# Tables and projection in one stage, four stored blocks a side, masks and picking rows kept on chip

## The reference

```python
xn = layernorm(x)
q, k, v = xn @ Wq + bq, xn @ Wk + bk, xn @ Wv + bv          # 16 heads of 16
pos = rel_emb @ Wk + bk                                     # 128 rows: one for a bucket of distance
scores = q @ k.T + take(q @ pos.T, c2p_pos) + take(k @ pos.T, p2c_pos).T
out = (softmax(scores / sqrt(48)) @ v) @ Wo + bo + xn
x = x + layernorm(layernorm(out) * ln_scale + ln_bias)
# feed-forward: expert = argmax(layernorm(x) @ Wr + br); relu(. @ W1 + b1) @ W2 + b2; again norm and residual
```

## Time and profile before

| | us |
|---|---|
| median of 3 runs (1906.63 to 1910.41) | 1906.98 |
| the profiled execution | 1909.95 |
| its span, first to last instruction | 1908.0 |
| TensorE busy | 1656.5 (87%) |
| DVE busy | 1390.5 (73%) |
| ScalarE busy | 1151.0 (60%) |
| GpSimd busy | 1071.8 (56%) |
| data moved by DMA | 452.57 MB, 237 GB/s |

### The profile page before, as it was taken

How to read it: one execution, slowest core, us unless ns; L and a number is a source line. 1 busy time by engine, 2 the same in 40 slices (tenths; PEclk the granted TensorE clock), 3 DMA queues, 4 the chain that set the end, 5 groups by cost and what they waited for, 6 DMA issues and landing times. The chain is left out here.

```text
span 1908.0 us, 41019 instructions
## 1 busy us (share of the span) xinstructions
PE 1656.5 (87%) x13688; PEld 1140.5 (60%) x13688; DVE 1390.5 (73%) x3938; ACT 1151.0 (60%) x2745; POOL 1071.8 (56%) x1268
## 2 busy tenths in 40 slices
PE   1883289999999999999999999999944755999997
PEld 1442056666666666666666666666523645999996
DVE  1573099999999999999999999999823652434343
ACT  1673258888888888887887888888622540222221
POOL 0210187787787787787787787787403521333332
PEclk9997589999999999999999999999976765999998
DMA  3599788878788878778888778878259823676772
GB/s 106 183 301 306 221 287 285 282 261 286 259 259 291 281 258 287 262 257 289 286 257 282 267 257 278 270 258 278 64 126 275 268 76 137 210 215 215 224 211 74
DMA packets 320830, 452.57 MB, mean 237 GB/s; under 512 B 38204, under 2 KB 260303, under 8 KB 320526
## 3 DMA queue, kind: packets, MB, share of 16 engines
q1 hardware_dynamic: 308034, 414.42, 67.6%
q10 hardware_dynamic: 7596, 21.10, 3.6%
q0 software_dynamic: 4992, 14.43, 2.1%
HBM read 256.87 MB, written 193.27 MB: 236 GB/s over the span
## 5 line engine op out<-in xcount | busy, mean ns | idle before, releaser
L872 ACT ACTIVATE t_probsT<-t_flip 128x512 f32<-128x512 f32 x1024 | 626.2, 614 | 200.3 <-PE t_flip L766 141.8
L817 DVE TENSOR_REDUCE t_most<-t_scores 128x1 f32<-128x640 f32 (+1 forms) x512 | 435.4, 850 | 58.1 <-PE t_scores L743 54.5
L836 DVE TENSOR_SCALAR t_band<-t_band,t_top 128x384 f32<-128x384 f32 (+1 forms) x512 | 415.5, 812 | 0.0
L780 PE MATMUL t_sum_ps<-t_probsT,t_vals 128*32 128x256 f32 x4096 | 327.2, 391 | 0.2 <-ACT t_probsT L872 0.2
L864 ACT COPY t_table<-t_table_ps 128x388 f32<-128x388 f32 x512 | 247.9, 484 | 65.3 <-issue 40.9
L949 POOL TENSOR_TENSOR t_near<-t_near,t_masks 128x768 f32<-128x768 f32 (+1 forms) x128 | 270.4, 2113 | 0.0
L821 DVE CUSTOM_DVE_ANT_0 t_band<-t_scores,t_near 128x384 f32<-128x384 f32 (+1 forms) x512 | 262.0, 512 | 0.0
L766 PE MATMUL t_flip<-t_masks,t_band 128*128 128x128 f32 x1408 | 260.6, 274 | 0.0
L736 PE MATMUL t_scores<-t_after,t_quest 105*128 105x256 bf16 (+3 forms) x1024 | 243.3, 287 | 3.8 <-DVE t_most L821 3.6
L743 PE MATMUL t_scores<-t_masks,t_near 128*128 128x128 f32 x1408 | 241.1, 274 | 1.6 <-POOLq L952 1.5
L743 PEld LDWEIGHTS t_scores<-t_masks,t_near 128*128 128x128 f32 x1408 | 180.7, 142 | 40.9 <-POOLq L952 2.8
(11 more groups left out here) (187 smaller groups left out, 2569.7 us busy)
## 6 DMA issues: line engine op xcount, KB each, us to landing
skew_d<-t_table SPq DMA_DIRECT2D x128, 1024.0 KB, 7.1
t_near<-skew_d SPq DMA_DIRECT2D x128, 640.0 KB, 8.1
t_near<-skew_d SPq DMA_DIRECT2D x128, 384.0 KB, 6.4
e_w<-in_L_ffn_W_dram ACTq DMA_DIRECT2D x39, 512.0 KB
e_w<-in_L_ffn_W_dram SPq DMA_DIRECT2D x39, 512.0 KB
split_d<-p_part SPq DMA_DIRECT2D x32, 384.0 KB
t_after<-split_d SPq DMA_DIRECT2D x64, 192.0 KB
t_quest<-split_d SPq DMA_DIRECT2D x64, 192.0 KB
```

Source lines behind the costliest of these rows:

```text
L780: last = nc.tensor.matmul(sum_ps[32 * g:32 * g + 32, 0:2 * P], vals[b % 2][:, j, h * VDIM:h * VDIM + 32], probsT[s % 3][:, g * 2 * P:(g + ...
L817: nc.vector.tensor_reduce(most[:, c, 1:2], out[:, wide:S], AX.X, ALU.max)
L836: nc.vector.tensor_scalar(band[n % 2][:, t, 0:wide], band[n % 2][:, t, 0:wide], top[n % 2][:, t:t + 1], None, ALU.subtract).then_inc(level ...
L872: nc.scalar.activation(probsT[s % 3][:, half * 512:(half + 1) * 512], flip_ps[half][:, :], ACT.Exp, scale=SCALE).then_inc(expd, 1)
```

## The change

`spread` is gone; its work is done inside `project`, on banks of PSUM that are not yet in use: the position rows first, then the first group of x, with the later passes of the tables between the norms. `far_w` is written straight into its place on chip. The 24 transfers of the picking rows follow the loads on SP, and they are read back into the SBUF tensor `rows` during the projection, which outlives the stage; so do `masks` and `inv_all`, the inverse deviations of all 32 tiles.

Of the six slots a side only four different blocks are stored: for q the first part twice, then the second and the third; for k the three parts, then the second again. A unit reads each side in two transfers of 48 rows, each with an outermost count of 3 (for k one of them has step 0 and reads one block three times), and the rows of the picking tables are put in the order that this gives. Per group there are 8 stores of parts instead of 12. `far_d` is stored in one transfer a group, padding rows included, and read for two units at a time. Nothing is stored for the residual: `mix` computes x times `inv_all` plus the projection on DVE, tile by tile. The diff's TensorE lines add only bo there, as a matmul with one row of ones.

```diff
 TERMS = 6
 VDIM = DH + 1
 VROW = (H + 1) * VDIM - 1
-QSLOTS = ((0, 1, 3), (3, 1, 2), (5, 1, 1))
-KSLOTS = ((1, 2, 3), (2, 2, 2), (0, 1, 1))
+BLOCKS = 4
+QSLOTS = ((0, 3, 4), (1, 5), (2,))
+KSLOTS = ((0, 1, 2), (3, 5), (4,))
...
-        xn_d = dram("xn_d", [TOK, D])
-        split_d = dram("split_d", [2, TERMS, N * DH, S], BF16)
-        far_d = dram("far_d", [2, N, 2, PARTS, S], BF16)
+        split_d = dram("split_d", [2, BLOCKS, N * DH, S], BF16)
+        far_d = dram("far_d", [B, 4, 32, PARTS, S], BF16)
         v_d = dram("v_d", [TOK, VROW])
         pick_d = dram("pick_d", [KROWS, H * 2 * FEW], BF16)
         skew_d = dram("skew_d", [2 * P * 2 * QT * 2 * P + 2 * P])
-        posT_d = dram("posT_d", [P, 2 * 2 * 8])
         ctx_d = dram("ctx_d", [N, P, 2 * P])
         share_d = dram("share_d", [N, S])
         rows_d = dram("rows_d", [TOK, 2 * D])
         bias_d, total_d = dram("bias_d", [E, HID]), dram("total_d", [E, D])
 
-        spread(nc, sem, Wk, bk, rel_emb, c_pick, c_masks, c_side, pick_d, posT_d)
-        spent = sem.spend()
-        project(nc, sem, spent, x, Wq, bq, Wk, bk, Wv, bv, bo, c_masks, posT_d, xn_d, split_d, far_d, v_d)
-        sem.take_back(spent)
-        spent = sem.spend()
-        attend(nc, sem, spent, c_masks, split_d, far_d, v_d, pick_d, skew_d, ctx_d)
+        masks = ctx.enter_context(nc.sbuf_tensor("masks", [P, 5, P], F32))
+        inv_all = ctx.enter_context(nc.sbuf_tensor("inv_all", [P, NT], F32))
+        with nc.sbuf_tensor("rows", [KROWS, H, 2, FEW], BF16) as rows:
+            project(nc, sem, x, Wq, bq, Wk, bk, Wv, bv, rel_emb, c_pick, c_masks, c_side, pick_d, split_d, far_d, v_d,
+                    masks, inv_all, rows)
...
-def spread(nc, sem, Wk, bk, rel_emb, c_pick, c_masks, c_side, pick_d, posT_d):
...
-            load(0)
-            for semaphore in spent:
-                sp.sem_clear(semaphore)
-            loads = [(masks[:, :, :], c_masks),
-                     (wq[:, :, :], Wq.rearrange("(k p) n -> p k n", p=P)),
-                     (wk[:, :, :], Wk.rearrange("(k p) n -> p k n", p=P)),
+            front = [(rel[:, :], rel_emb), (masks[:, :, :], c_masks), (wk[:, :, :], Wk.rearrange("(k p) n -> p k n", p=P)),
+                     (bk_row[:, :], bk.rearrange("(a n) -> a n", a=1)), (side[:, :, :], c_side),
+                     (pick[:, 0, :], c_pick[0, :, :]), (pick[:, 1, :], c_pick[1, :, :])]
+            assert len(front) == 7
+            loads = [(wq[:, :, :], Wq.rearrange("(k p) n -> p k n", p=P)),
                      (wv[:, :, :], Wv.rearrange("(k p) n -> p k n", p=P)),
                      (bqk[:, 0:2], bq.rearrange("(c p) -> p c", p=P)),
                      (bqk[:, 2:4], bk.rearrange("(c p) -> p c", p=P)),
-                     (bv_b[:, :], view(bv.tensor, 0, [[0, P], [1, D]])),
-                     (bo_b[:, :], view(bo.tensor, 0, [[0, P], [1, D]]))]
-            assert len(loads) == 8
+                     (bv_b[:, :], view(bv.tensor, 0, [[0, P], [1, D]]))]
+            assert len(loads) == 5
+            load(0)
+            for dst, src in front:
+                sp.dma_start(dst, src, allow_slow_non_contiguous=True).then_inc(front_in, 16)
             for dst, src in loads:
                 sp.dma_start(dst, src, allow_slow_non_contiguous=True).then_inc(loaded, 16)
-            sp.wait_ge(padded, 1)
-            sp.dma_start(far_w[:, :, 0:16], posT_d[:, :].rearrange("p (c s) -> p c s", c=2)).then_inc(loaded, 16)
             for g in range(1, XB):
                 load(g)
-            for s in range(-2, NG + 1):
-                g = s + 2
-                if live(g):
-                    sp.wait_ge(xnb_made, g + 1)
-                    sp.dma_start(view(xn_d, g * G * D, [[D, P], [P * D, GT], [1, D]]), xnb[g % 2][:, :, :]
-                                 ).then_inc(xn_out[g % 2], 16)
-                    if live(g + XB):
-                        load(g + XB)
+            sp.wait_ge(pos_act, 6)
+            sp.wait_ge(pos_dve, 3)
+            for tab in range(2):
+                for n, slots in enumerate((KSLOTS, QSLOTS)[tab]):
+                    for slot in slots:
+                        for c in range(2):
+                            sp.dma_start(view(pick_d, slot * (DH * H * 2 * FEW) + c * 8 * 2 * FEW + tab * FEW,
+                                              [[2 * FEW, 8], [H * 2 * FEW, DH], [1, FEW]]),
+                                         pick_part[:, n, tab, c, :]).then_inc(pick_out, 16)
...
                     sp.wait_ge(lo_made, g + 1)
                     for m in range(4):
-                        for n, (first, step, many) in enumerate((QSLOTS, KSLOTS)[m // 2]):
-                            at = ((m // 2 * TERMS + first) * (N * DH) + b * D + m % 2 * P) * S + half * G
-                            sp.dma_start(view(split_d, at, [[S, P], [step * N * DH * S, many], [1, G]]),
-                                         part[g % 2][:, n, m, :].unsqueeze(1).to_broadcast([P, many, G])
-                                         ).then_inc(split_out[g % 2], 16)
+                        mine = at + m // 2 * (BLOCKS * part_at) + m % 2 * (P * S)
+                        takes = ((0, 3, 1), (0, 1, 0)) if m < 2 else ((0, 3, 0), (1, 2, 3))
+                        for a, z, slot in takes:
+                            sp.dma_start(view(split_d, mine + slot * part_at, [[S, P], [part_at, z - a], [1, G]]),
+                                         part[g % 2][:, a:z, m, :]).then_inc(split_out[g % 2], 16)
                     sp.wait_ge(far_lo_made, g + 1)
-                    for m in range(4):
-                        at = (m // 2 * N + b * H + m % 2 * 8) * 2 * PARTS * S + half * G
-                        sp.dma_start(view(far_d, at, [[PARTS * S, 16], [S, PARTS], [1, G]]),
-                                     far_part[g % 2][32 * m:32 * m + 16, :, :]).then_inc(far_out[g % 2], 16)
+                    sp.dma_start(view(far_d, b * (P * PARTS * S) + half * G, [[PARTS * S, P], [S, PARTS], [1, G]]),
+                                 far_part[g % 2][:, :, :]).then_inc(far_out[g % 2], 16)
                 g = s
                 if live(g):
                     sp.wait_ge(v_kept, g + 1)
                     sp.dma_start(view(v_d, g * G * VROW, [[VROW, P], [P * VROW, GT], [1, VROW]]), v32[g % 2][:, :, :]
                                  ).then_inc(v_out[g % 2], 16)
+                if s == 2:
+                    sp.wait_ge(pick_out, 16 * 4 * TERMS)
+                    sp.dma_start(rows[:, :, :, :].rearrange("p h a v -> p (h a v)"), pick_d[:, :]).then_inc(rows_in, 16)
...
+            act.wait_ge(pos_pe, 1)
+            nc.scalar.copy(relT[:, :, :], far_ps[:, 0:2 * P].rearrange("p (c r) -> p c r", c=2)).then_inc(pos_act, 1)
+            act.wait_ge(pos_pe, 2)
+            nc.scalar.copy(pos[:, :], far_ps[:, 2 * P:4 * P]).then_inc(pos_act, 1)
             for s in range(-2, NG + 1):
                 ahead, g, back = s + 2, s, s - 1
+                if s == -1:
+                    keep_x(0)
...
+                if s == -2:
+                    act.wait_ge(pos_pe, 3)
+                    nc.scalar.copy(posT[:, :, :], far_ps[:, 0:2 * P].rearrange("p (c r) -> p c r", c=2)[:, :, 0:P:P - 1]
+                                   ).then_inc(pos_act, 1)
+                    for tab in range(2):
+                        last = nc.scalar.copy(pick32[:, tab, :, :], v_ps[:, 2 * tab:2 * tab + 2, 0:FEW])
+                    last.then_inc(pos_act, 1)
+                    act.wait_ge(pos_act, 4)
+                    nc.scalar.copy(pick_part[:, 0, :, :, :], pick32[:, :, :, :]).then_inc(pos_act, 1)
+                if s == -1:
+                    act.wait_ge(pos_dve, 2)
+                    nc.scalar.copy(pick_part[:, 1, :, :, :], pick_rest[:, :, :, :]).then_inc(pos_act, 1)
...
-            pe.wait_ge(loaded, 16 * 9)
+            ident = masks[:, 4, :]
+            pe.wait_ge(front_in, 16 * 7)
+            for c in range(2):
+                last = nc.tensor.transpose(far_ps[:, c * P:(c + 1) * P], rel[:, c * P:(c + 1) * P], ident)
...
+            last.then_inc(pos_pe, 1)
             turn(0)
+            pe.wait_ge(loaded, 16 * 5)
...
-        @block.gpsimd
-        def _(pool):
-            pool.wait_ge(loaded, 16 * 9)
-            for g in range(NG):
-                pool.wait_ge(xn_made, GT * (g + 1))
-                if g >= 2:
-                    pool.wait_ge(xn_out[g % 2], 16 * (g // 2))
-                nc.gpsimd.tensor_tensor(xnb[g % 2][:, :, :], xn[g % NB][:, :, :],
-                                        bo_b[:, :].unsqueeze(1).to_broadcast([P, GT, D]), ALU.add).then_inc(xnb_made, 1)
...
-    HATS = 5
+    HATS = 4
+    FARS = 2
+    ROW = DH * PARTS
...
-        quest, after, before = ([sb(f"{w}{i}", [ROWS, S], BF16) for i in range(BUFS)] for w in ("quest", "after", "before"))
-        rows = sb("rows", [KROWS, H, 2, FEW], BF16)
+        quests, afters, befores = (sb(w, [ROWS, BUFS, S], BF16) for w in ("quests", "afters", "befores"))
```

(46 more changed lines are left out.)

217 lines of the change are left out of this document (81 added, 136 removed).

## The result

The changed kernel takes 1873.26 us (median of 4 runs, 1872.12 to 1876.15) against 1906.81 for the kernel before: a ratio of 0.982, 95% interval 0.981 to 0.984. The forecast was 1868; the measured time lies inside its range, and the change is faster as forecast.

| stage | before | after | measured | predicted |
|---|---|---|---|---|
| start of attention, after tables and projection | 195.6 | 136.2 | -59.4 | -57.6 |
| attention | 1201.0 | 1216.7 | +15.7 | +26 |
| mix, to the first gather of the experts | 195.8 | 209.5 | +13.6 | -6 |
| experts, to the end of the span | 315.5 | 309.4 | -6.1 | -1 |
| span | 1908.0 | 1871.8 | -36.2 | -38.6 |

The account below looks back on a forecast made before the run. Attention was taken as bound by TensorE, the projection by written bytes. Terms -57.6 + 0 + 26 - 6 - 1 = -38.6 us took the profiled 1909.95 to 1871.4, less 3.0 to the median: 1868 us, range 1838 to 1910.

Parts of the forecast that it names:

- Front: Tables and projection joined into one stage: it ends near 138 against 195.6 us, -57.6 us, bounds -37 and -62.
- the cover of the table stores: At the front: table stores on SP end near 39.4, before first parts near 42; uncovered they cost at most 14.85 us.
- written bytes: Projection stage before the change: said to be bound by them, 9.75 us a group on 12 stores at 327 GB/s.
- Reads: Reads of the parts in attention: outermost count 3 for 6 makes three DMA engines the bound, +26 us, bounds 0 and +75.
- Three engines: Part reads in attention: outermost count sets the engines, so three for six, taking 5.5 us a unit instead of 2.75.
- the price of 0.4 us a unit: Attention: 18.1 us of traffic on the three engines against a period of 17.69, over 62 units.
- the start of attention that I had put at 0: Start of attention: ScalarE's table copies and their queue are untouched, so 0, bounds -4 and +4 us.
- Mix: Mix stage: normalised rows no longer read, against the added bias work: -6 us, bounds -15 and +10.
- the bias row: Mix stage: one-row matmul a tile takes a group from 3.78 to 5.7 us at half clock; mostly covered, +0.5 us.
- the five steps: Mix stage, from 1455 to 1495 us: DMA paces them, 8 us each; normalised rows no longer read there give -4.5 us.
- Experts: Experts stage: 0.33 MB of masks leaves the loads the first matmul waits for, -1 us, bounds 0 and -2.
- the last step of the sum: From 1871.4 to 1868 us: the old profiled execution stood 3.0 us above its median of 1906.98.

## Why the prediction was right in the whole and off in its parts

**Front, right in size, wrong in one reason.** -59.4 for -57.6. The first projection, the cover of the table stores and the groups of 12.39 us came as worked out. But the late groups of before were not bound by written bytes alone, as I had it: six blocks with the same 12 transfers cost 4.6 us, the store of x with GpSimd's pass 6.4, and both together 18.6. That GpSimd's hold on DVE is the way by which the second acts is likely from the rows and not shown by a run.

**Reads, cause right, price too high, +15.7 for +26.** Three engines, their share, their rate and GpSimd's wait were right. The mis-sized term is the price of 0.4 us a unit: I compared 18.1 with 17.69, a mean over 61 distances that holds the last four short ones, where no tables are made. The steady pace of before is 17.82 over 57 distances. (18.04 - 17.82) x 57 = 12.4 us, and 3.4 us go before the first sum (94.8 us after the stage begins, for 91.4), in the start of attention that I had put at 0. That the mean of 18.04 lies so near the 18.1 is in part luck: I had every unit at 18.1, and most take 17.82 while a few behind loads of values take much more.

**Mix, +13.6 for -6, the wrong sign, and beyond its bound of +10.** The mis-sized term is the bias row, at +0.5. I counted 1.9 us more a group and called it covered by the DMA pace, and I priced it at clocks seen in the old trace. What the runs showed: this row was worth 24.0 us, of which 21.4 come back when the same matmul has 128 rows; that is the clock for the larger part (12 us or more), and the longer one-row pair for the rest. The bound was miscounted too: of 16 groups, 11 and not nine lie outside the five steps, and 11 x 1.9 - 6.5 is 14. The rest of the term had the right sign and was too small: without bo the stage is 10.3 us below before, for 6.5.

**Experts, -6.1 for -1.** The masks' load weighed some 3 us and not 1, and some 3 us are unexplained.

The errors (-2, -10, +20, -5) add up to +2.4 us. That the whole came out so near is luck: the +20 of the mix stage happens to stand against 17 us the other way. The other 3 of the 5.3 us between 1868 and 1873.3 come from the last step of the sum, which took off 3.0 us because the old profiled execution stood so far above its median; the new one stood 0.4 above its own.

Three smaller slips of the working change nothing: 129 + 6.5 + 1.2 + 2 is 138.7, not 138; (18.1 - 17.69) x 62 is 25, not 26; and masks and picking rows together are 0.9 MB, not 1.5.

## What to carry to other kernels

Read a steady period from a stretch without its ends before a margin of a few tenths is judged. Write the access pattern of a read so that its outermost count is not small (3 gave 3 engines here, 6 gave 6; 16 cost attention 13 us less than 3), above all where the reads share queues with traffic that is near full. A small matmul added to a stage must be priced by what it does to the granted clock as well as by its time: padding the one-row f32 matmul to 128 rows made its pair shorter (1.06 us for 1.22 at 1.2 GHz) and gave 21 us of the stage back. A mean that agrees with a forecast proves little until the single periods have been looked at.

## What the runs showed of the hardware that I had not expected

- An f32 matmul with one row took 1.22 us a pair at 1.2 GHz, with 128 rows 1.06; with one row among them TensorE stayed at 1.2 GHz through 52 us of unbroken work, and with 128 rows the same 52 us of the stage had a mean granted clock of 0.89.
- A DVE pass of 0.69 us took 2.85 when it met a GpSimd pass of 2.90 on SBUF.
- Right behind the issue of a load of 1.18 MB, an issue on SP that otherwise takes 0.56 us took 5.47.
- Six blocks with 12 stores a group ran at 367 GB/s, mean from 60 to 130 us, where the kernel before had 288 to 331 GB/s in stretches of 10 us from 100 to 150 us.
